# A three-stage decoder block on one core: reordered beginning, bias folds as rows, joined outputs of the last pair

## The reference

```
x = layernorm(x + attn(x))          # stage A
x = layernorm(x + xattn(x, ctx))    # stage B
x = layernorm(x + ffn(x))           # stage C

attn:  Q, K = x@wq+bq, x@wk+bk; prep(t) = tanh(t@w1 + b1)@w2 + b2  (16 heads of 16)
       qe, ke = rotations of prep(Q), prep(K) mixed over the first sequences
       s = |qe|^2 * |ke|^2; attn = softmax(s / s); out = attn@V @ wo + bo
xattn: two softmaxes per head, softmax(q1 k1) - gain * softmax(q2 k2); per-head norm; @ wo.T
ffn:   logits = x@router_w + ..., two of four experts, softmaxed, weigh
       e0 = silu(x@sw_w1) * (x@sw_w3) @ sw_w2
       e1 = gelu(((x@me_eq_w+b)@me_wv+b)@me_wo+b)@me_c1w+b) @ me_c2w + b
       e2 = post-norm block: syn = x@ce_syn_w+b, attn = (syn@ce_wv+b)@ce_wo+b,
            two layernorms, relu(h@ce_f1w+b)@ce_f2w+b, @ce_gen_w+b
       e3 = gelu(x@ml_w1+b) @ ml_w2 + b
```

## Time and profile before

| | us |
|---|---|
| median of 3 runs | 1577.65 |
| lowest, highest | 1576.88, 1582.46 |
| profiled execution | 1578.52 |
| its span, first to last instruction | 1576.7 |
| PE busy | 1512.6 (96%) |
| DVE busy | 1141.8 (72%) |
| ACT busy | 846.3 (54%) |
| POOL busy | 367.2 (23%) |
| mean granted PE clock | 0.98 of full |

### The profile page before, as it was taken

The page is one execution under the profiler, slowest core; times in us unless marked ns, Lnnn a source line. Parts: engine busy times, 40 slices in busy tenths (PEclk is TensorE's granted clock), DMA queues, the critical chain, the costliest instruction groups (busy, mean ns, idle before and its releaser), DMA issues.

```text
span 1576.7 us, 28790 instructions
## 1 busy us (share of the span) xinstructions
PE 1512.6 (96%) x11272; PEld 1074.4 (68%) x11272; DVE 1141.8 (72%) x2311; ACT 846.3 (54%) x1121; POOL 367.2 (23%) x399
## 2 busy tenths in 40 slices
PE   6999999888899999999999899999999999999998
PEld 3333333334566666666657788898989888898887
DVE  5445556557899999999964787777676777777675
ACT  4888889764688888888863232222222122222221
POOL 0000001121645666666451220000000000000000
PEclk9999999987999999999998999999999999999999
DMA  7656665454465665656642100000000000000000
GB/s 148 136 109 117 124 119 104 70 93 92 70 112 89 104 97 93 110 77 97 96 157 68 61 1 14 1 1 14 1 15 1 14 1 14 1 3 12 1 14 14
DMA packets 61574, 97.23 MB, mean 62 GB/s; under 512 B 12588, under 2 KB 29880, under 8 KB 61440
## 3 DMA queue, kind: packets, MB, share of 16 engines
q1 hardware_dynamic: 61440, 95.41, 32.6%
HBM read 26.16 MB, written 4.19 MB: 19 GB/s over the span
## 4 chain that ended last, share of the span: by engine, by line
PE 89%; DVE 7%; ACT 3%; issue 1%; POOL 0%; DMA 0%; POOLq 0%; DVEq 0%; ACTq 0%
PE ps L109 84%; PE ps L1163 2%; ACT PX L1317 1%; ACT H L555 1%; DVE EE L676 1%; DVE NM L1372 1%; PE ps L1125 1%; PE ps L1171 1%; DVE XC L1977 1%; PE ps L1785 0%; PE ps L1095 0%; PE ps L1776 0%; DVE XH L590 0%; DVE X L601 0%; DVE X L752 0%
## 5 line engine op out<-in xcount | busy, mean ns | idle before, releaser
L1372 DVE TENSOR_REDUCE NM<-ps 128x4 f32<-128x1024 f32 x256 | 307.7, 1219 | 35.8 <-PE ps L109 34.3
L1317 ACT ACTIVATE PX<-ps 128x1024 f32<-128x1024 f32 x256 | 262.2, 1024 | 79.7 <-PE ps L109 78.7
L555 ACT ACTIVATE H<-ps,b1c 128x1024 f32<-128x1024 f32 x256 | 268.3, 1118 | 39.7 <-PE ps L109 38.1
L1937 ACT ACTIVATE GF<-ps,cols 128x512 f32<-128x512 f32 x128 | 88.2, 689 | 295.6 <-PE ps L109 295.5
L109 PE MATMUL ps<-XC,W_sw_w 128*128 128x512 f32 x768 | 187.4, 395 | 0.0
L109 PEld LDWEIGHTS ps<-XC,W_sw_w 128*128 128x128 f32 x768 | 141.6, 190 | 28.4
L2128 DVE CAST GH<-GF 128x512 fp32r<-128x512 f32 x192 | 81.9, 427 | 106.9 <-ACT GF L1937 101.7
L2236 POOL TENSOR_SCALAR RSc<-AGc 128x4 f32<-128x4 f32 x23 | 6.9, 300 | 602.2 <-DVE AGc L2023 602.2
L109 PE MATMUL ps<-PX,VT 128*32 128x256 f32 x2048 | 139.6, 391 | 0.1
L1932 ACT ACTIVATE GF<-ps 128x512 f32<-128x512 f32 x64 | 38.1, 595 | 189.0 <-PE ps L109 189.0
L2130 DVE TENSOR_TENSOR GH<-GF,GH 128x512 fp32r<-128x512 f32 x192 | 133.2, 694 | 6.6
(11 more groups left out here) (233 smaller groups left out, 2560.1 us busy)
## 6 DMA issues: line engine op xcount, KB each, us to landing
ST<-QS SPq DMA_DIRECT2D x256, 96.0 KB, 2.8
KT<-KS SPq DMA_DIRECT2D x128, 192.0 KB, 4.7
QT<-XSb SPq DMA_DIRECT2D x128, 96.0 KB, 4.1
XT<-in_xT_dram SPq DMA_DIRECT2D x8, 512.0 KB, 4.3
raw_a<-in_x_dram SPq DMA_DIRECT2D x8, 512.0 KB, 4.3
CR<-in_ctxT_dram SPq DMA_DIRECT2D x8, 512.0 KB, 4.3
out_dram<-X SPq DMA_DIRECT2D x7, 512.0 KB, 3.0
R_sw_w<-in_sw_w_dram SPq DMA_DIRECT2D x6, 512.0 KB, 5.3
```

Source lines behind the costliest of these rows:

```text
L555: e.activation(H1[s % 8][:, :, :], PP[s % 3][:, :, :], ACT.Tanh, bias=b1c[:, half:half + 1], scale=1.0).then_inc(act_th, 1)
L1317: e.activation(PX[s % 3][:, :, :, :], PP[2][:, :, :].rearrange("p g (c q) -> p g c q", c=2), ACT.Exp, bias=0.0, scale=0.25).then_inc(act_e ...
L1372: e.tensor_reduce(NM[u % 2][:, qc, :, :, i], PP[qc][:, :, :].rearrange("p g (m k) -> p g m k", m=2), AX.X, ALU.max, negate=True).then_inc( ...
L1937: e.activation(g[:, :], o, f, bias=cols[:, col:col + 1], scale=1.0).then_inc(act_g, 1)
```

## The change

In stage A POOL first clears a tile, `zero`, and PE runs 18 matmuls on it into bank 5 before its first projection. ACT runs tanh on one column after its sine, and then starts two of tile 0's gathers (c = 1, h = 1 and 3) from its own queue; SP starts the other 14, in another order. DVE stores the projections of tile 1 and splits the second x before it clears TA, MM, BO and computes cs. In period 0 PE projects tile 2 after w1(2) and w1(3).

In stage B the last pair's outputs are two calls, at steps 267 and 275, that fill bank 6, and DVE adds 512 columns at once. The bias fold becomes two: f = 12 (step 256, bank 4) multiplies each of the four biases, repeated in 32 columns, by rows of 512 of its matrix, 8 matmuls in four column groups; DVE copies the 512 columns; f = 13 (step 258, bank 5) multiplies 128-column blocks of this by a 128x2 selector that adds the groups, 4 matmuls. What waited for 13 folds waits for 14. The selector and the repeated biases are laid out on the host as `vb` (258 columns for 8). In stage C the first pair's synergy uses the banks (2, 3, 6, 7).

```diff
+    zero = H1[7][:, 0, :]
+    def first_stack(e, w, c, heads):
+        w.wait_ge(dve_qs, 2 * c + 2)
+        w.wait_ge(pool_hi, c + 1)
+        for h in heads:
+            dma(e, f32(ST[0][64 * c:64 * c + 48, h, :]), f32(QS0[16 * h:16 * h + 16, c, :, :]), d_s0[h // 2])
 phase_a, sync
-        for k in range(4):
-            for c in range(2):
-                w.wait_ge(dve_qs, 2 * c + 2)
-                w.wait_ge(pool_hi, c + 1)
-                for h in (2 * k, 2 * k + 1):
-                    dma(e, f32(ST[0][64 * c:64 * c + 48, h, :]), f32(QS0[16 * h:16 * h + 16, c, :, :]), d_s0[k])
+        for c, heads in ((0, (0, 1, 2)), (1, (0, 2)), (0, (3, 4, 5)), (1, (4, 5)), (0, (6, 7)), (1, (6, 7))):
+            first_stack(e, w, c, heads)
 phase_a, tensor
+        w.wait_ge(pool_zero, 1)
+        for i in range(18):
+            mm(e, P[5][0:16, 0:128], zero[:, 0:16], zero[:, 0:128], True, True)
         free0 = project(0, 0, 6, none)
...
-            if pr is not None:
+            if pr is not None and J:
                 free[7] = project(*pr, 7, free[7])
...
             for r in range(2, 4):
                 if J < NJ:
                     w1(4 * J + r)
+            if not J:
+                free[7] = project(*pr, 7, free[7])
 phase_a, scalar
         e.activation(trg[:, :, :], ang[:, :, :], ACT.Sin, bias=0.0, scale=1.0).then_inc(act_trig, 1)
+        e.activation(SQ[:, 0:1], ang[:, 0, 0:1], ACT.Tanh, bias=0.0, scale=1.0)
+        first_stack(e, w, 1, (1, 3))
 phase_a, vector
+        for c in range(2):
+            project(1, c, 6 + c)
+        for k in range(2):
+            split_x(1, k)
         e.memset(TA[:, :], 1.0).then_inc(dve_init, 1)
...
-        for k in range(2):
-            split_x(1, k)
...
-        for c in range(2):
-            project(1, c, 6 + c)
 phase_a, gpsimd
+        one.done(e.memset(zero[:, :], 0.0), pool_zero)
 phase_b
-                p = due(s, 41 + 8 * b + 4 * qc, 32, NP)
+                p = due(s, 41 + 8 * b + 4 * qc, 32, NP - 1)
                 if p is not None:
-                    return p, b, qc
+                    return p, b, (qc,)
+            if s == NS + 11 + 8 * b:
+                return NP - 1, b, (0, 1)
...
-        return due(s, NS - 12, 1, 13)
+        return 13 if s == NS + 2 else due(s, NS - 12, 1, 13)
 phase_b, tensor: output
+            for k, qc in enumerate(halves):
+                for c in range(2):
+                    t = mm3(e, P[6][:, 256 * k:256 * k + 256], OH[:, b, c, 0, qc, :], OH[:, b, c, 1, qc, :], wo[:, c, 0, :], wo[:, c, 1, :],
+                            k == 0 and c == 0, c == 1)
 phase_b, tensor: fold
-                for col in range(8):
-                    at = 128 * (col % 4)
-                    for v, m in ((0, R2), (1, R1), (2, T["me_c1w"])) if col < 4 else ((3, T["ce_f1w"]),):
-                        for k in range(2):
-                            t = mm(e, P[b][:, col:col + 1], m[:, k, at:at + 128], vb[:, v, k:k + 1], col == 0 and v == 0 and k == 0, True)
+            elif f == 12:
+                for k in range(2):
+                    for v, m in enumerate((R2, R1, T["me_c1w"], T["ce_f1w"])):
+                        t = mm(e, P[b][32 * v:32 * v + 32, :], rows4[:, v, k, :], m[:, k, :], k == 0, k == 1)
+            else:
+                w.wait_ge(dve_fold, 13)
+                for c in range(4):
+                    t = mm(e, P[b][:, 2 * c:2 * c + 2], BS[:, 128 * c:128 * c + 128], sums, c == 0, True)
 phase_b, vector
+                w.wait_ge(pe_out, tile + n)
+                x2 = X1[:, tile:tile + n, :]
+                e.tensor_tensor(x2, x2, P[6][:, 0:256 * n].rearrange("p (v f) -> p v f", v=n), ALU.add).then_inc(dve_x2, n)
...
+                elif f == 12:
+                    t = e.tensor_copy(BS, o)
                 else:
-                    t = e.tensor_tensor(cols[:, 0:8], cols[:, 0:8], o[:, 0:8], ALU.add)
+                    c8 = cols[:, 0:8].rearrange("p (x c) -> p c x", x=2)
+                    t = e.tensor_tensor(c8, c8, o[:, 0:8].rearrange("p (c x) -> p c x", x=2), ALU.add)
 phase_c
+def syn_banks(j):
+    return (2, 3, 6, 7) if j == 0 else (7, 6, 2, 3)
```

More of the change, by code:

```diff
@@ L273, in phase_a @@
     pool_rs = M.sem("a_pool_rs")
+    pool_zero = M.sem("a_pool_zero")
     pool_seq = M.pool_seq
@@ L845, in phase_b @@
     RS = put("RSb", [128, 4])
-    FB = Place(M, 0)("FB", [128, 8976])
+    FB = Place(M, 0)("FB", [128, 9228])
     br = Place(M, 143360)("br", [128, 3, 256])
@@ L860, in phase_b @@
     vc = FB[:, n + 512:n + 1024].rearrange("p (v k n) -> p v k n", v=2, k=2)
-    vb = FB[:, n + 1024:n + 1032].rearrange("p (v k) -> p v k", v=4)
-    v2 = FB[:, n + 1032:n + 1288].rearrange("p (k n) -> p k n", k=2)
+    v2 = FB[:, n + 1024:n + 1280].rearrange("p (k n) -> p k n", k=2)
+    vb = FB[:, n + 1280:n + 1538]
+    rows4 = vb[:, 0:256].rearrange("p (v k m) -> p v k m", v=4, k=2)
+    sums, BS = vb[:, 256:258], T["me_eqT"].rearrange("p k n -> p (k n)")
     PRODUCTS = ((RI, T["ce_wvT"], T["ce_wo"], 256, 0), (R1, T["me_woT"], T["me_c1w"], 512, 0), (Wce, T["ce_synT"], RI, 256, 2),
@@ L1173, in turn_n, with output @@
             free[7] = (dve_oh, u + 1)
-        def output(p, b, qc):
+        def output(p, b, halves):
             w.wait_ge(dve_oh, 4 * p + 3 + b)
@@ L1178, in output @@
             w.wait_ge(*free[6])
-            for c in range(2):
-                t = mm3(e, low, OH[:, b, c, 0, qc, :], OH[:, b, c, 1, qc, :], wo[:, c, 0, :], wo[:, c, 1, :], c == 0, c == 1)
-            t.then_inc(pe_out, 1)
+            for k, qc in enumerate(halves):
+                for c in range(2):
+                    t = mm3(e, P[6][:, 256 * k:256 * k + 256], OH[:, b, c, 0, qc, :], OH[:, b, c, 1, qc, :], wo[:, c, 0, :], wo[:, c, 1, :],
+                            k == 0 and c == 0, c == 1)
+            t.then_inc(pe_out, len(halves))
             free[6] = (dve_x2, 4 * p + 2 * b + qc + 1)
         def fold(f):
-            b = f % 2 if f < 12 else 4
-            if f == 12:
+            b = f % 2 if f < 12 else f - 8
+            if f >= 12:
                 w.wait_ge(act_ex, NS)
@@ L1353, in step @@
             if o is not None:
[L1354 to L1357, removed]
+                p, b, halves = o
+                n = len(halves)
+                tile = 4 * p + 2 * b + halves[0]
+                w.wait_ge(pe_out, tile + n)
+                x2 = X1[:, tile:tile + n, :]
+                e.tensor_tensor(x2, x2, P[6][:, 0:256 * n].rearrange("p (v f) -> p v f", v=n), ALU.add).then_inc(dve_x2, n)
             o = turn_o_due(s - 1)
@@ L1417, in step @@
             if f is not None:
-                o = P[f % 2 if f < 12 else 4]
+                o = P[f % 2 if f < 12 else f - 8]
                 w.wait_ge(pe_fold, f + 1)
@@ L1564 @@
 EARLY = {259: 0, 262: 1, 264: 2, 266: 3, 268: 4, 270: 5, 274: 6, 278: 7, 282: 8, 288: 9, 294: 10}
-SYN_BANKS = (7, 6, 2, 3)
 GEN_BANKS = (7, 6, 0, 1)
@@ L1721, in early @@
             if s == 259:
-                w.wait_ge(b_end["folds"], 13)
+                w.wait_ge(b_end["folds"], 14)
             if s == 278:
@@ L1759, in synergy @@
             wt = W["ce", 0]
-            for i, b in enumerate(SYN_BANKS):
+            for i, b in enumerate(syn_banks(j)):
                 if b > 3:
@@ L2408, in col @@
         return Fn[name].reshape(-1, 128).T
-    r["vb"] = np.stack([col(k) for k in ("me_eq_b", "me_bv", "me_bo", "ce_n1b")], 1)
+    vb = np.stack([col(k) for k in ("me_eq_b", "me_bv", "me_bo", "ce_n1b")], 1)
+    sums = np.stack([(p % 32 == 0) & (p < 96), p == 96], 1).astype(f)
+    r["vb"] = np.concatenate([np.repeat(vb.reshape(128, 8), 32, 1), sums], 1)
     r["vc"] = np.stack([np.repeat(col(k)[:, :, None], 128, 2) for k in ("ce_syn_b", "ce_bv")], 1)
```

## The result

The changed kernel takes 1568.23 us (median of four, 1567.17 to 1569.30). The kernel before, timed beside it, takes 1580.06 (1576.88 to 1584.27): ratio 0.9924, 95% interval 0.9895 to 0.9952. It is faster, as forecast, but the 1559 was 9 us too low and the time lies 0.2 us outside the range 1553 to 1568. Its profiled run took 1567.9, span 1566.1, mean clock 0.977.

What follows compares the result with a forecast made beforehand. TensorE (PE), busy 96% of the span, was taken as the bound. Start 4.1, fold 6.3, clock and banks 3.2, outputs 4.8 sum to 18.4 off 1578.5, giving 1560.1; median 0.9 lower: 1559 us, range 1553 to 1568.

Steps and rivals of the forecast that it cites:

- From there PE is dense and the lead stays: After PE's combine near 43 us: the 4.1 us gained at the beginning is kept to the end.
- rival F: Whole span: PE falls to the low clock at added waits, 0.38 us lost per us low; slower, 1586 us; chance 0.02.
- Start, -4.1: First 50 us: dummies, two gather queues and new order bring PE's combine from 47.19 to 43.05; bounds 2.9 and 6.5.
- a sign of being wrong: Beginning: the prediction is wrong if w1(16), and not DVE's QS of tile 3, is held by ST.
- Rival D: Beginning: dummies don't raise the clock and overrun to 10.8 us, lead at combine falls to 1.5; 1562 us; chance 0.09.
- Rival C: Beginning: SP isn't the limit, so 6.5 us gained instead of 4.1, and no NTl wait; 1555 us; chance 0.11.
- Fold, -6.3: Bias product after cross attention: 9.1 us on PE becomes 1.9 for eight matmuls plus 0.9 to 1.2 for four.
- rival E: Bias fold: column groups run one after the other, 5 us of the passage's gain lost; 1564 us; chance 0.03.
- Clock and banks, -3.2: turn_o and synergy behind the fold: 3.6 us at full clock, wait for PR hidden, instead of 6.8.
- just free: Synergy would start at 845.5 us, W_me's last split having ended at 845.44, so no wait for it.
- Outputs, -4.8: Outputs before the feed-forward stage: waits of 5.2 us go, 2.0 us NTl wait comes, 1.6 us of low clock goes.
- Rival B: Passage bound by DVE: outputs gain nothing and the start gives 2.9 us; 1565 us; chance 0.23.

Runs made afterwards that it cites:

- again_after: The changed kernel unedited, run and profiled once more: 1567.33 us, ratio 0.9885 to the kernel before.
- part_passage: The kernel before with only the edits from the bias fold on (two-part fold, joined outputs, synergy's banks), old start: 1570.74 us, ratio 0.9916.
- two_again: The changed kernel unedited, run again beside later combined versions: 1566.48 us, ratio 0.9901 to the kernel before.
- t_turn: The changed kernel with the last turn_n moved from step 271 to 275 and the last output from 275 to 279: 1565.41 us, ratio 0.9882 to the kernel before.
- f_rep2: The changed kernel with the maxima's matmuls issued three times in each of the first 31 steps: 1565.92 us, ratio 0.9904 to the kernel before.
- part_fold: The kernel before with the two-part bias fold alone, outputs and order of banks as before: 1577.80 us.

## Why the prediction was right or wrong

**The failed step: the middle stood in the sum at nothing, with "2 to 3 us for where the clock's low stretches fall" in the range.** "From there PE is dense and the lead stays" is not so in the middle: from 392 to 416 us PE was busy for 20.94 of 24 us in the kernel before, it waits for ACT and DVE again and again, and in this part of the span the clock falls. How long it stays low differs between executions of one kernel. Of 13 profiles of kernels without added work, those of before and after among them, nine have 54.6 to 61.4 us low and four have 34 to 44. The kernel before, on whose first profile the sum was made, is there among the four. The middle took 144.3 to 153.9 us accordingly, from again_after (37.5 low, 144.33) to part_passage (61.4 low, 153.94): 0.40 us for each microsecond low between these two, 0.35 by a straight line through all 13, 0.38 in rival F. The range held 2 to 3 us for this; the runs showed 9.6.

**The base was part of the same step.** The kernel before takes 1582.4 to 1584.66 us in the four later comparisons (medians of 8 to 17 runs each), not 1577.65. Against those medians the change gives 17.3 (again_after) and 15.9 (two_again), where 18.4 was forecast. On a base of 1583 the sum would have given 1564.6, less than 3 us below again_after and two_again; the other 5.6 of the 9 us are the well drawn base. So the lead is not lost as a rule: part_start, which has the new start alone, is 5 us faster over twelve runs (interval 1.6 to 8.7), and the first pair of profiles drew a good middle for the kernel before and a bad one for the changed kernel. Rival F's mechanism did act, at +5.7 us in that pair, but the change does not bring it. That the measured time fell outside the range was a draw too: 1568.23 is 0.2 above its upper end, and the medians of again_after and two_again lie inside.

**Start, -4.1: 3.6.** Right in the dummies (3.00 us, forecast 3.1), in the path (QS of tile 3 held by ST until 41.18, forecast 40.7) and at combine (43.43, forecast 43.05). Wrong in SP's gain, 1.93 and not 2.75: of the gathers on SP two stretched to 0.89 and 1.04 us while ACT's two were in flight, so 14 ended at 21.12, not 20.3; the two on ACT's queue gave some 0.4 us, not 1.25. w1 starts at 17.46, not at 16.0, as its last wanted gather lands later, with tanh at 18.23; that cost nothing, since the path goes by tile 3. By the Trainium skill, "DMA: Bandwidth & Descriptors", section "Issuing engines are not separate DMA queues", the second queue would save only its sequencer's time; the rows agree in part: two queues lifted 157 to 183 GB/s with the engines 0.85 and then 0.93 busy, and the gathers on both slowed down. In some executions w1(16) waits too, until tile 1's gathers have landed (1.40 us in again_after, 1.59 in t_turn, none in the changed kernel's first profile), and a low stretch follows; there the lead at 52 us is 2.3 and 1.2 instead of 3.7. This is the wait that the prediction had named as a sign of being wrong, and it costs: over the seven profiles with this start (two gathers on ACT, with dummies) the start ended between 293.19 and 295.89, on average at 294.2, which is 2.6 before the average of the four with the old start and not 4.1. Rival D is out: the dummies ended at 6.69. Rival C is out with two gathers on ACT; six of them reach 292.33, 1.1 more.

**Fold, -6.3: 6.5.** In the changed kernel it holds PE for 1.83 and 0.81 us (844.99 to 846.82, 850.65 to 851.46) where it was 9.10. The 16 records take 1.90, as in the row of w2; rival E is out.

**Clock and banks, -3.2: 3.0.** turn_o and synergy took 3.83 us (846.82 to 850.65) instead of 6.82. Synergy itself took 3.10 and waited 0.23 for W_me, "just free" being 0.23 short.

**Outputs, -4.8: 3.1.** This is what is left of the 12.6. The 3.05 and the 1.75 went. The wait for NTl was 2.47 (forecast 2.0), and behind it the low clock, which I had put away with the wait for OH, came back: chunk 6 took 4.58 us and not 2.94, a term of 1.6 us that the sum lacks. t_turn shows its size: without the wait 2.94, and 3.9 us less in all. It too is a draw: in seven of the nine profiles with this wait the chunk behind it took 4.31 to 4.59 us, in part_passage and f_rep2 it took 3.02 and 3.04, and part_passage's tail is shorter by the 14.3 us of the forecast. Rival B would have left nothing to outputs; part_fold, whose tail is 6.0 us longer than the changed kernel's (745.2 to 739.15), puts it out, although its 1565 lies nearer to the result than my 1559.

| | forecast | profiles |
|---|---|---|
| start | -4.1 | -3.6 |
| middle | 0 | +5.7 |
| passage | -14.3 | -12.7 |
| sum | -18.4 | -10.6 |

**Open.** What decides the draw of the middle. It is not the new start (part_passage lacks it) nor the time at which PE comes into attention (part_start and the changed kernel differ by 0.04 us there and by 5.1 in the middle), and more matmuls don't cure it. No experiment here took away the waits in the middle themselves.

## What to carry to other kernels

A profile is one draw of the granted clock, and so are three runs. Before a sum is made on it, look in its windows for stretches below full clock, and give the range 0.4 us for each microsecond by which they may grow. After each wait that a change adds on PE, allow for slower matmuls behind it (here 1.6 us behind a wait of 2.5, in seven profiles of nine), and take them off again where a wait goes. And look whether the path that you shorten has a second wait close behind it, as w1(16) was here.

## What the hardware showed

Low clock came back in the middle of the span, 300 us after the start, in all profiles, and the changed kernel's middle took 144.3 to 153.2 us for it between executions. The Trainium skill, "TensorE: Matmul & The Clock Gate", Part 1, section "What's actually happening", calls the number of slow matmuls at a kernel's start variable from run to run and the penalty of the ramp under 1% of a typical span. The rows agree that it varies; but it varies far behind the start too, and the spread there over all kernels without added work, 9.6 us, is 0.6% of the span, half of what this whole change gave. Two DMA queues with small gathers (96 KB, 48 rows of 2 KB) gave 183 GB/s against 157 from one. Matmuls of one column were followed by a fall of the clock without any idle time of PE before it (granted 1.00 from 842 to 848 us and 0.50 from there on, while the fold ran from 842.99 to 852.09; with the fold as rows it was 1.00 from 842 to 852), and their 64 records took 9.24 us in one execution and 11.99 in another.
